# The order of turns, value products and projection pieces in the wide attentions of a four-layer kernel

## The chip, the core and the metric

The kernel runs on one core of a Trainium2 chip. The metric is the device time of one execution in microseconds. The core's engines are TensorE (PE for its matmuls, PEld for its weight loads), VectorE (DVE), ScalarE (ACT), GpSimd (POOL) and the DMA queues started by SyncE (SP).

## What is computed

Four layers, each a cross attention to a context followed by a mixture of experts or feed-forward network, on 16 batches of 112 tokens of width 256; the context has 375 rows. The change concerns the attentions of layers 2 and 3, cut here to their core (layer 3 adds biases to q, k, v and the output):

```python
qh = (q @ Wq).reshape(B_, Sq, 16, 64).transpose(0, 2, 1, 3)
kh = (k @ Wk).reshape(B_, Sk, 16, 64).transpose(0, 2, 1, 3)
vh = (v @ Wv).reshape(B_, Sk, 16, 64).transpose(0, 2, 1, 3)
scores = jnp.einsum('bhqd,bhkd->bhqk', qh, kh) / jnp.sqrt(jnp.float32(D_K))
attn = jax.nn.softmax(scores, axis=-1)
ctx = jnp.einsum('bhqk,bhkd->bhqd', attn, vh)
return ctx.transpose(0, 2, 1, 3).reshape(B_, Sq, 1024) @ Wo
```

## The kernel before

`cross_attention` emits one stage for each of layers 0, 2 and 3. In layers 2 and 3 the heads are 64 wide, so `EC`, the number of 128-row blocks of keys, is 8 and `wide` is true; in layer 0 it is false. There is no scheduler: each engine has a function of its own that walks the batches and heads in an order written out by hand, and semaphores tie them together.

For each batch and **pair** of heads (h even, h + 1) TensorE does these things:

- **scores** (S, L470): six matmuls of 376 columns, for both heads, into the two banks `psS`. It waits until ACT's exponentials have emptied both banks.
- **turn** (T, L497): three transposes that turn one head's weighted probabilities into the one bank `psT`. It waits for GpSimd's weighing of that head (`weighed`) and for ACT's copy of the previous head's turn (`probsT_ready`), since there is one bank.
- **pair_values** (PV, L512): twelve matmul records, the product of the turned probabilities of two heads with the values.
- **pieces** (`piece`, from L389): projections for the next batch and the output product of the last one. K0 to K7 are blocks of keys (six matmuls of 376 columns, L416), V0 to V5 blocks of values (six of 512 columns, L423), Q0 and Q1 queries (L408), L0 and L1 two transposes of the normed tokens (L401), Y0 and Y1 the output product of the batch before (L451). The dictionary `order` tells behind which head each stands.

Before the change a pair reads on TensorE, with h even:

S(h, h+1), T(h-3), pieces of h, T(h-2), PV(h-4, h-3), pieces of h+1.

The eight pairs of a batch hold these pieces, those of h before the bar and those of h+1 behind it: K0 K1 | K2; K3 | L0 L1 K4; V0 | V1; Y0 | V2; Y1 | K5; Q0 | V3; Q1 | V4; K6 | V5 K7.

The other engines, per pair: DVE takes the two maxima (`head_max`, L866). ACT copies T(h-3) (`take_probsT`, L654), exponentiates h and h+1 (L674), takes the pieces of h, copies T(h-2), and takes the pieces of h+1. GpSimd weighs every head (`weigh`): the inverse of the sum (L716), then the multiplication by it (L718). At head 8 it first starts the gathers of expert rows for a later batch (`gather`, L736): two in layer 2, one in layer 3, for the first twelve batches.

A K piece goes through two engines. ACT writes its high part (`keys_hi`, L626) and DVE then its low part (`keys_lo`, L808), and only then is its bank free. K pieces alternate between two banks of their own, so K2 waits for DVE to be done with K0, and K4 for K2. In the first pair DVE also starts the norm of the next batch (`normalise_start`) behind the maxima and ahead of K0. In the second pair, behind the maxima, it ends it (`normalise_end`, L788), and L0 waits for that.

What the four `probs` and four `probsT` buffers are read by sets the distances: T three and two heads behind the scores, PV four behind.

## Time and profile before

| | us |
|---|---|
| median of 3 runs | 3487.58 |
| lowest and highest | 3485.43, 3488.54 |
| the profiled execution | 3493.50 |
| its span, first to last instruction | 3491.7 |
| stage of layer 2's heads | 1515.9 to 2201.0 of the span |
| stage of layer 3's heads | 2477.7 to 3173.2 of the span |

The profile is of one execution. A timeline row has the start in microseconds from the start of the span, the duration, the engine, the line, the operation, what it writes from what, the shape, how many instructions were merged, and in brackets idle time of the engine before it with what ended it. The end of a matmul is modelled, so distances on TensorE are taken from start to start. A windows row has the stretch, its length, the busy time of PE, PEld, DVE, ACT and POOL with instruction counts, the granted TensorE clock as a share of the full one, the DMA share and GB/s.

### The profile page before, as it was taken

To read this page: it belongs to the slowest core of one execution; us is meant where nothing else is said; L and a number is where in the kernel's file an instruction comes from. 1 tells how busy PE (TensorE), PEld (TensorE's weight loads), DVE (VectorE), ACT (ScalarE), POOL (GpSimd) and SP (SyncE) were. 2 spreads that over 40 slices of the span, in tenths; PEclk is the share of its full clock that TensorE was granted. 3 is DMA by queue.
4 is the path that set the end of the run, shared out by engine and by line. 5 is a ranking of instruction groups with operands and counts; after the bars stand their busy time and mean duration, and the time that the engine had idled before them with its cause. 6 is when DMAs were issued, how large, how long until landed. Compare 5 with 4: busy or idle time off the path is not lost. (4 is left out here: it accounts for less than half of the span.)

```text
span 3491.7 us, 60671 instructions
## 1 busy us (share of the span) xinstructions
PE 3171.1 (91%) x21982; PEld 2617.9 (75%) x21982; DVE 1555.4 (45%) x3343; ACT 1527.9 (44%) x4145; POOL 1308.9 (37%) x1417
## 2 busy tenths in 40 slices
PE   5888869998989869989999999699899999996999
PEld 4777758996666646668888887588788888875998
DVE  4777750004566520044444444300444444445766
ACT  2555524443355512245555555234455555552332
POOL 0000001113100011057777776310577777773343
PEclk8999959999999879999999999699999999997999
DMA  6556536542100234110000000298000000001433
GB/s 145 131 133 137 118 130 204 182 166 82 38 1 1 88 93 119 60 32 15 15 15 15 15 13 1 77 320 276 27 13 13 13 13 13 11 1 44 120 103 90
DMA packets 154741, 269.25 MB, mean 77 GB/s; under 512 B 50396, under 2 KB 129753, under 8 KB 140393
## 3 DMA queue, kind: packets, MB, share of 16 engines
q1 hardware_dynamic: 140840, 239.95, 23.2%
q0 software_dynamic: 8064, 20.20, 2.2%
q10 hardware_dynamic: 5568, 5.51, 0.5%
q8 instruction: 172, 2.82, 0.3%
q14 instruction: 97, 0.79, 0.1%
HBM read 231.13 MB, written 34.46 MB: 76 GB/s over the span
## 5 line engine op out<-in xcount | busy, mean ns | idle before, releaser
L718 POOL TENSOR_SCALAR L_probs<-L_probs,L_inverse 112x375 f32<-112x375 f32 x512 | 653.0, 1275 | 119.5 <-issue 119.5
L866 DVE TENSOR_REDUCE L_negmax<-bank 112x1 f32<-112x375 f32 x768 | 394.6, 542 | 431.7 <-PE bank L470 356.9
L674 ACT ACTIVATE L_probs<-bank,L_negmax 112x375 f32<-112x375 f32 x768 | 435.2, 572 | 219.6 <-DVE L_negmax L866 214.7
L497 PE MATMUL bank<-ident,L_probs 112*125 112x112 f32 x2304 | 399.6, 282 | 21.2 <-POOL L_probs L718 15.4
L497 PEld LDWEIGHTS bank<-ident,L_probs 112*125 112x125 f32 x2304 | 338.8, 190 | 92.6 <-issue 50.9
L716 POOL TENSOR_TENSOR L_inverse<-L_sums,neg_one 112x1 f32<-112x1 f32 x512 | 297.1, 580 | 142.2 <-ACT L_probs L674 141.8
L654 ACT ACTIVATE L_probsT<-bank 125x336 f32<-125x336 f32 x512 | 231.9, 453 | 248.1 <-PE bank L497 248.1
L636 ACT ACTIVATE v<-bank 125x512 f32<-125x512 f32 x192 | 114.8, 598 | 267.4 <-PE bank L423 267.4
L704 POOL TENSOR_TENSOR L_stats<-L_stats,neg_half 112x1 f32<-112x1 f32 x48 | 27.1, 564 | 517.7 <-DVE L_stats L783 517.7
L512 PE MATMUL bank<-L_probsT,v 125*64 125x112 f32 x3072 | 206.1, 269 | 2.4 <-ACT L_probsT L654 1.1
L416 PE MATMUL bank<-L_ctx_hi,L_wk_hi 128*128 128x376 f32 x512 | 149.3, 373 | 29.8 <-DVE L_ctx_lo L850 22.1
L512 PEld LDWEIGHTS bank<-L_probsT,v 125*64 125x64 f32 x3072 | 151.5, 137 | 31.5 <-issue 2.7
L1582 ACT ACTIVATE L0t_hidden<-bank,L0t_b 128x128 f32<-128x128 f32 x280 | 102.3, 367 | 143.1 <-PE bank L1547 125.4
L674 ACT ACTIVATION_READ_ACCUMULATOR L_probs<-bank,L_negmax 112x1 f32 x768 | 152.9, 199 | 0.0
L1547 PEld LDWEIGHTS bank<-L0t_xT,L0t_w 128*128 128x128 f32 x1120 | 133.3, 195 | 5.9 <-issue 4.2
L423 PE MATMUL bank<-L_wv_hi,L_ctx_hi 128*125 128x512 f32 x384 | 137.7, 440 | 0.0
L1547 PE MATMUL bank<-L0t_xT,L0t_w 128*128 128x128 f32 x1120 | 133.8, 279 | 3.5 <-DMA L0t_w<-in_F_w 2.4
L808 DVE SCALAR_TENSOR_TENSOR L_keys_lo<-bank,L_bk,L_keys_hi 128x376 fp32r<-128x376 f32 x128 | 76.4, 606 | 130.8 <-ACT L_keys_hi L626 130.8
L416 PE MATMUL bank<-L_ctx_hi,L_wk_lo 128*128 128x376 f32 x512 | 131.6, 339 | 0.0
L416 PE MATMUL bank<-L_ctx_lo,L_wk_hi 128*128 128x376 f32 x512 | 131.3, 338 | 0.0
L1520 POOL DMA_INDIRECT L0t_xs<-tokens,rows_of x35 | 33.4, 955 | 256.6 <-PE bank L1533 209.7
L1598 DVE TENSOR_TENSOR L0t_ys<-bank,L0t_b 128x256 f32<-128x256 f32 x35 | 14.9, 424 | 253.9 <-PE bank L1559 253.9
(305 smaller groups left out, 6968.0 us busy)
## 6 DMA issues: line engine op xcount, KB each, us to landing
L2t_w<-in_F_w SPq DMA_DIRECT2D x42, 1024.0 KB, 5.1
L0t_w<-in_F_w SPq DMA_DIRECT2D x35, 1024.0 KB, 5.0
L_keys<-spread_k SPq DMA_DIRECT2D x64, 376.0 KB, 6.4
L_ctxT<-in_ctxT SPq DMA_DIRECT2D x48, 375.0 KB, 3.3
tile_w<-in_F_w SPq DMA_DIRECT2D x16, 1024.0 KB, 5.8
L3d_row<-comb_rows SPq DMA_DIRECT2D x64, 224.0 KB, 3.3
w_all<-in_F_w SPq DMA_DIRECT2D x8, 1024.0 KB, 13.6
L_q<-spread_q SPq DMA_DIRECT2D x128, 56.0 KB, 2.2
```

The source lines that it names most:

```text
L416: ins = pe.matmul(bank[:, 0:SP], wt[:, k, m * P:(m + 1) * P], c[b.par][:, k, :], start=(n + k == 0), stop=(n + k == DC + 1))
L423: ins = pe.matmul(bank[0:SJ, 0:VW], c[b.par][:, k, j * SJ:(j + 1) * SJ], wt[:, k, vn * VW:(vn + 1) * VW], start=(n + k == 0), stop=(n + k ...
L497: ins = pe.transpose(psT[h % len(psT)][0:SJ, j * T:(j + 1) * T], probs[h % NB][:, j * SJ:(j + 1) * SJ], core.ident[0:T, 0:T])
L512: ins = pe.matmul(bank[i * dh:(i + 1) * dh, at:at + T], v[b.par][0:SJ, j, (h + i) * dh:(h + i + 1) * dh], probsT[(h + i) % NT][:, j, :], s ...
L636: ins = act.activation(v[b.par][0:SJ, j, n * VW:(n + 1) * VW], bank[0:SJ, 0:VW], ACT.Copy)
L654: act.activation(probsT[h % NT][:, :, :], psT[h % len(psT)][0:SJ, 0:J * T].rearrange("p (j t) -> p j t", t=T), ACT.Copy)\
L674: act.activation(probs[e % NB][:, :], psS[e % 2][0:T, 0:S], ACT.Exp, bias=negmax[b.par][:, e:e + 1], accum_out=sums[b.par][:, e:e + 1]).th ...
L716: pool.tensor_tensor(inverse[b.par][:, h:h + 1], sums[b.par][:, h:h + 1], core.neg_one[0:T, :], ALU.pow)
L718: pool.tensor_scalar(probs[h % NB][:, :], probs[h % NB][:, :], inverse[b.par][:, h:h + 1], None, ALU.mult)\
L866: dve.tensor_reduce(negmax[b.par][:, h:h + 1], psS[h % 2][0:T, 0:S], AX, ALU.max, negate=True).then_inc(maxed.sem, 1)
L1547: ins = pe.matmul(psH[f % 4][:, 0:tile], w1[t % 2][:, k, f * P:(f + 1) * P], xT[:, k, :], start=(k == 0), stop=(k == DC - 1))
L1582: act.activation(hidden[:, f, :], psH[f % 4][:, 0:tile], func, bias=b1[:, bass.ds(e, 1), f:f + 1].rearrange("p a f -> p (a f)"))\
```

## The change

In wide attentions only:

- Both turns of a pair stand behind the scores with one value product between them. A pair reads S(h, h+1), T(h-3), PV(h-6, h-5), T(h-2), then the pieces of h and those of h+1.
- The value product is of a pair two heads older than before. The tail gets one more product for that.
- ACT copies T(h-2) between the two exponentials, where it stood behind the pieces of h.
- In `order` the first half of the second pair becomes L0 L1, and K3 and K4 stand together behind them. All other pairs keep their pieces. DVE's and GpSimd's functions are not edited.

```diff
     if wide:
-        order = {0: ["K0", "K1"], 1: ["K2"], 2: ["K3"], 3: ["L0", "L1", "K4"], 4: ["V0"], 5: ["V1"], 6: ["Y0"],
+        order = {0: ["K0", "K1"], 1: ["K2"], 2: ["L0", "L1"], 3: ["K3", "K4"], 4: ["V0"], 5: ["V1"], 6: ["Y0"],
                  7: ["V2"], 8: ["Y1"], 9: ["K5"], 10: ["Q0"], 11: ["V3"], 12: ["Q1"], 13: ["V4"],
                  14: ["K6"], 15: ["V5", "K7"]}
...
                         scores(b, h)
-                        if not (b_first and h < lag):
+                        if wide and h % 2 == 0:
+                            if not (b_first and h < 3):
+                                turn(*before(b, h, 3))
+                            if not (b_first and h < 6):
+                                pair_values(*before(b, h, 6))
+                            if not (b_first and h < 2):
+                                turn(*before(b, h, 2))
+                        if not wide and not (b_first and h < lag):
                             turn(*before(b, h, lag))
-                        if wide and h % 2 == 1 and not (b_first and h < 5):
-                            pair_values(*before(b, h, 5))
...
                     if wide:
                         turn(b, H - 3)
+                        pair_values(b, H - 6)
                         turn(b, H - 2)
                         pair_values(b, H - 4)
...
-                        if wide and not (b_first and h < lag):
-                            take_probsT(*before(b, h, lag))
+                        if wide and h % 2 == 0 and not (b_first and h < 3):
+                            take_probsT(*before(b, h, 3))
 
                         for e in ((h, h + 1) if h % 2 == 0 else ()) if wide else (h,):
+                            if wide and e == h + 1 and not (b_first and h < 2):
+                                take_probsT(*before(b, h, 2))
                             act.wait_ge(maxed.sem, maxed.at(H * b.n + e + 1))
```

TensorE in the second pair of a batch before the change. L497 is a turn, L512 the value product, L401 the transposes L0 and L1, L416 with `wk_hi` and `wk_lo` a K piece:

```order
L470 MATMUL bank<-L_keys_hi,L_q_low 112x376 x2
L497 MATMUL bank<-ident,L_probs 125x112 x3
L416 MATMUL bank<-L_ctx_hi,L_wk_hi 128x376 x2
L416 MATMUL bank<-L_ctx_lo,L_wk_hi 128x376 x2
L416 MATMUL bank<-L_ctx_hi,L_wk_lo 128x376 x2
L497 MATMUL bank<-ident,L_probs 125x112 x3
L512 MATMUL bank<-L_probsT,v_3 64x112 x6
L401 MATMUL bank<-ident,L_normed 128x112 x2
L416 MATMUL bank<-L_ctx_hi,L_wk_hi 128x376 x2
```

The same place after the change:

```order
L470 MATMUL bank<-L_keys_hi,L_q_low 112x376 x2
L497 MATMUL bank<-ident,L_probs 125x112 x3
L512 MATMUL bank<-L_probsT,v_3 64x112 x6
L497 MATMUL bank<-ident,L_probs 125x112 x3
L401 MATMUL bank<-ident,L_normed 128x112 x2
L416 MATMUL bank<-L_ctx_hi,L_wk_hi 128x376 x2
L416 MATMUL bank<-L_ctx_lo,L_wk_hi 128x376 x2
L416 MATMUL bank<-L_ctx_hi,L_wk_lo 128x376 x2
L416 MATMUL bank<-L_ctx_hi,L_wk_hi 128x376 x2
```

K3, which stood ahead of L0, now stands behind L1, and nothing but the two turns and the product stands between the scores and L0.

ACT over the first two pairs of a batch before the change: L654 is the copy of a turn, L674 the exponential, L626 the high part of a K piece, L624 the copy of L0 and L1:

```order
L654 ACTIVATE L_probsT<-bank 125x336
L674 ACTIVATE L_probs,L_sums<-bank,L_negmax 112x375 x2
L626 ACTIVATE L_keys_hi<-bank 128x376 x2
L654 ACTIVATE L_probsT<-bank 125x336
L626 ACTIVATE L_keys_hi<-bank 128x376
L654 ACTIVATE L_probsT<-bank 125x336
```

After it, with the line numbers of the changed kernel (L660 copy of a turn, L682 exponential, L632 high part of a K piece):

```order
L660 ACTIVATE L_probsT<-bank 125x336
L682 ACTIVATE L_probs,L_sums<-bank,L_negmax 112x375
L660 ACTIVATE L_probsT<-bank 125x336
L682 ACTIVATE L_probs,L_sums<-bank,L_negmax 112x375
L632 ACTIVATE L_keys_hi<-bank 128x376 x3
L660 ACTIVATE L_probsT<-bank 125x336
```

The second copy of a turn moved from behind the pieces of h to between the exponentials, and the three K pieces of the first pair are taken in a row.

## Rows read from the trace of the kernel before

**Rows 1.** Windows of layer 2's and layer 3's head stages.

```profile
1515.90:2201.00 685.10, 671.28 (x5267) 547.69 (x5269) 312.30 (x647) 359.50 (x999) 492.80 (x543) 1.00 0.05 13
2477.70:3173.20 695.50, 681.64 (x5354) 557.14 (x5354) 315.93 (x635) 376.83 (x1008) 502.57 (x555) 0.99 0.04 10
```

**Rows 2.** Timeline of PE, layer 3, first two pairs of the sixth batch.

```profile
2693.84 0.43 PE L470 MATMUL bank<-L_keys_hi,L_q_high 64*112 64x376 f32 x2
...
2694.53 0.58 PE L497 MATMUL bank<-ident,L_probs 112*125 112x112 f32 x3
2694.88 0.60 PE L416 MATMUL bank<-L_ctx_hi,L_wk_hi 128*128 128x376 f32 x2
...
2696.00 0.51 PE L416 MATMUL bank<-L_ctx_hi,L_wk_hi 128*128 128x376 f32 x2
...
2697.03 0.48 PE L497 MATMUL bank<-ident,L_probs 112*125 112x112 f32 x3
2697.45 0.80 PE L512 MATMUL bank<-L_probsT,v 125*64 125x112 f32 x12
2698.17 0.62 PE L416 MATMUL bank<-L_ctx_hi,L_wk_hi 128*128 128x376 f32 x2
...
2699.40 0.42 PE L470 MATMUL bank<-L_keys_hi,L_q_high 64*112 64x376 f32 x2
...
2701.96 0.80 PE L512 MATMUL bank<-L_probsT,v 125*64 125x112 f32 x12
2702.69 0.41 PE L401 MATMUL bank<-ident,L_normed 112*128 112x112 f32 x2
...
2704.07 0.42 PE L470 MATMUL bank<-L_keys_hi,L_q_high 64*112 64x376 f32 x2
```

**Rows 3.** Timeline of PE, layer 2, first pair of the sixth batch.

```profile
1736.58 0.43 PE L470 MATMUL bank<-L_keys_hi,L_q_high 64*112 64x376 f32 x2
...
1741.15 0.62 PE L416 MATMUL bank<-L_ctx_hi,L_wk_hi 128*128 128x376 f32 x2 [0.16 <-DVE L_keys_lo L808]
...
1742.38 0.42 PE L470 MATMUL bank<-L_keys_hi,L_q_high 64*112 64x376 f32 x2
```

**Rows 4.** Timelines of ACT (layer 3), DVE (layer 3), DVE (layer 2), second pairs.

```profile
2700.71 0.45 ACT L654 ACTIVATE L_probsT<-bank 125x336 f32<-125x336 f32 x1 [0.63 <-PE bank L497]
...
2701.55 0.59 DVE L788 TENSOR_SCALAR L_normed<-x,L_stats 112x256 f32<-112x256 f32 x1
...
1744.38 0.40 DVE L788 TENSOR_SCALAR L_normed<-x,L_stats 112x256 f32<-112x256 f32 x1
```

**Rows 5.** Timelines of PE and DVE, K pieces in a row, layer 3's start, then layer 2's.

```profile
2459.10 0.61 PE L416 MATMUL bank<-L_ctx_hi,L_wk_hi 128*128 128x376 f32 x2 [0.29 <-DVE L_keys_lo L808]
...
2461.71 0.61 PE L416 MATMUL bank<-L_ctx_hi,L_wk_hi 128*128 128x376 f32 x2 [0.28 <-DVE L_keys_lo L808]
...
2461.04 0.61 DVE L808 SCALAR_TENSOR_TENSOR L_keys_lo<-bank,L_bk,L_keys_hi 128x376 fp32r<-128x376 f32 x1 [0.97 <-ACT L_keys_hi L626]
...
1498.53 0.62 PE L416 MATMUL bank<-L_ctx_hi,L_wk_hi 128*128 128x376 f32 x2
...
1501.00 0.61 PE L416 MATMUL bank<-L_ctx_hi,L_wk_hi 128*128 128x376 f32 x2
```

**Rows 6.** Timeline of PEld, layer 2's first batch: two turns with nothing between them.

```profile
1533.53 0.40 PEld L497 LDWEIGHTS bank<-ident,L_probs 112*125 112x125 f32 x3 [0.26 <-issue]
1534.71 0.40 PEld L497 LDWEIGHTS bank<-ident,L_probs 112*125 112x125 f32 x3 [0.78 <-POOL L_probs L718]
```

**Rows 7.** Timelines of PE and POOL, layer 2, sixth pair (heads 10, 11), two batches.

```profile
1763.11 0.42 PE L470 MATMUL bank<-L_keys_hi,L_q_high 64*112 64x376 f32 x2
...
1764.41 1.24 POOL L718 TENSOR_SCALAR L_probs<-L_probs,L_inverse 112x375 f32<-112x375 f32 x1 [2.29 <-issue]
...
1631.63 0.42 PE L470 MATMUL bank<-L_keys_hi,L_q_high 64*112 64x376 f32 x2
...
1631.69 1.24 POOL L718 TENSOR_SCALAR L_probs<-L_probs,L_inverse 112x375 f32<-112x375 f32 x1 [1.05 <-issue]
```

## The prediction, made before the changed kernel ran

> **What bounds the kernel now.** I read a window over each of the two stages that the change touches, then TensorE's timeline inside one batch. In the two stages TensorE is busy for 671.3 of 685.1 us and 681.6 of 695.5 us at a granted clock of 1.00 and 0.99 [rows 1]. GpSimd follows with 492.8 and 502.6 us. So nearly all of these 1380.6 us are TensorE's own work, and whatever the change does to the time it must do by the seams between TensorE's blocks or by new waits of TensorE. That is the upper of its two levels (2.4 GHz), so nothing is to be had from the clock.
>
> A timeline of TensorE, read from start to start, gives the price of each block with its seam. In layer 3's first pair: S 0.69 us, T 0.35, K0 1.12, K1 1.03, T 0.42, PV 0.72, K2 1.23, together 5.56 [rows 2]. The second pair takes 4.67 us: its PV starts at 2701.96 and L0 at 2702.69, again 0.73, and L0, L1, K4 take 1.38 up to the next scores [rows 2]. Layer 2's first pair takes 5.80 us, and its K2 is the one block that waits there: 0.16 us idle, ended by DVE's low part of K0 [rows 3].
>
> **The seams.** A turn behind the scores costs 0.58 us of modelled duration, one behind a K piece 0.48 [rows 2]: the first has 0.10 more because its weight loads do not run ahead. K0 behind a turn costs 1.12, K1 behind K0 1.03; K2 behind a value product has its first two matmuls in 0.62 where K1 has 0.51 [rows 2]. So a block in the wake of a turn or product pays about 0.1, and one behind a K piece does not.
>
> Before, the first pair pays at S-T, T-K, T-PV and PV-K, and K-T is free. After, it pays at S-T, T-PV, PV-T and T-K, and K-K is free. The seam PV-T does not occur in the rows, so I bound it. The nearest is PV-L0, another fp32 transpose with `ident`: 0.73 for the product with its seam [rows 2]. The other end is what the seam costs if the turn's load runs ahead as behind a K piece: the turn is then 0.10 cheaper, and the product's own 0.72 may shrink by about the same again. I take 0.72 and 0.10, the PV-L0 row being the same kind of instruction. Then the first pair is S 0.69, T 0.35 + 0.10 + 0.06 = 0.51 (a turn that leads to PV is 0.42 against 0.35, and this one also stands behind scores), PV 0.72, T 0.35, K0 1.12, K1 1.03, K2 1.23 - 0.11 = 1.12, in all 5.54 against 5.56. **The seams cancel.** The second pair comes out the same way at about 4.72 against 4.67, since K3 and K4 follow two small transposes. The other six pairs have V, Y or Q pieces at the same places; I take 0 for them, with 0.05 us either way per pair. Over six pairs and 30 batches (15 with pieces in each layer) that is 9 us up or down.
>
> **The copy of the first turn.** T(h-2) needs the one `psT` bank back, so ACT must have copied T(h-3). Before, a piece of over 1 us stood between them. Now the product does. In layer 2's first batch, where two turns stand back to back, the second one's weights load 1.18 us after the first's [rows 6]: that is turn, copy and signal. After the change the distance is 0.51 + 0.72 = 1.23 us. So the wait is covered, by 0.05 us. The copy starts 0.62 us behind its turn (2700.71 against 2699.40 + 0.69) and takes 0.45, and ACT sat idle for 0.63 us before it [rows 2, 4], so nothing stands in front of it. I cost it at 0, with up to 0.05 per pair, 12 us, as the upper end.
>
> **K2 in the first pair.** Three K pieces now stand in a row, and K2 needs K0's bank. Where K pieces stand in a row, the start of one to the start of the next but one is 2.61 us in layer 3 and 2.47 us in layer 2, ended by DVE's low part [rows 5]; without the wait it would be 1.12 + 1.03 = 2.15. Before, a turn and a product stood in between. K0 now starts 0.69 + 0.51 + 0.72 + 0.35 = 2.27 us into the pair, so K2 starts at 4.88 (layer 3) and 4.74 (layer 2), and with K2's 1.23 the pair takes 6.11 and 5.97 us. Against 5.56 and 5.80 [rows 2, 3] that is 0.55 and 0.17 us more, over 15 batches 8.3 + 2.6 = **10.9 us**. ACT copies T(h-2) from 1.92 + 0.62 = 2.54 to 2.99 us and has then the second exponential ahead of K0's high part, while K0 is made only at about 3.5 (2.27, 1.12 and some 0.1 for the last matmul to end, an estimate). I take it that ACT is there in time; if it were late by 0.1 us, that would be 3 us more.
>
> **L0 in the second pair.** L0 waits for DVE's normed tokens. In layer 3 these are done at 2701.55 + 0.59 = 2702.14 [rows 4], 2.74 us after the pair's start at 2699.40 [rows 2], and the signal from DVE to TensorE takes 0.06 us (DVE ends at 2461.65, the K piece starts at 2461.71 [rows 5]), so L0 can start at 2.80. Nothing on DVE ahead of that moves: K2's low part and the two maxima stand there before and after. Before, L0 came at 2702.69, 3.29 us in, and was safe. After, it would come at 0.69 + 0.51 + 0.72 + 0.41 = 2.33. It waits 0.47 us, and its weight load no longer runs ahead, 0.05. With the 0.05 of the seams the pair is 0.57 us longer. In layer 2 the tokens are done at 1744.78, 2.40 us into a pair that starts at 1742.38 [rows 3, 4]: a wait of 0.13, and 0.2 us in all. Together 15 x (0.57 + 0.2) = **11.5 us**.
>
> **T(8) behind the gathers, layer 2.** GpSimd weighs head 8 behind two gathers, and the multiplication ends 2.54 us after the scores of heads 10 and 11 start in one batch (1765.65 against 1763.11) and 1.30 us in another [rows 7]. Twelve batches have gathers, and these two are near the two ends of what they show. T(8) is the second turn of that pair. Before, it stood behind Q0, a piece longer than a microsecond. Now it stands at 0.69 + 0.51 + 0.72 = 1.92 us. It waits 0.68 in the one and nothing in the other; I take 0.46 on average, **5.5 us**, bounds 2 and 8. In layer 3, with one gather, I see no such wait.
>
> **What costs nothing.** S(h+2) waits for the second exponential. It now starts when the copy ends at 2.99, and the shortest pair is 4.67, which leaves 1.7 us. DVE's copies of the value products stand behind maxima that end later than the product. In the last batch of each stage, with few pieces, GpSimd sets the pace and the extra product in the tail lies in its shadow.
>
> **The sum.** 10.9 + 11.5 + 5.5 = 27.9 us more. Against the profiled execution's own 3493.5 that is 3521.4; against the median of 3487.6, which I forecast for, 3515.5, so about **3515**. From the bounds (seams -9 to +9, copy 0 to +12, T(8) -3.5 to +2.5, ACT 0 to +3) its own range is 3503 to 3530.
>
> **Rivals.** (a) *The product hides the turn's loads.* If TensorE loads T(h-2)'s weights while the product still runs, both ends of the seam PV-T shrink, 0.1 to 0.2 us for each of 240 pairs: 24 to 48 us less. With 36 us, the sum is -8 and the time 3480, faster by 0.23%. It decides the sign from 0.12 us per pair on. For it speaks that a K piece does hide a turn's loads [rows 2]; against it that the loads of K2 and L0 are not hidden behind a product. Chance 0.10. The Trainium skill (TensorE: Matmul & The Clock Gate, "Step-by-step: what each phase is for") says that the queue pulls weight loads ahead of matmuls in flight when the row groups don't conflict or the load goes to the background buffer; by that rule this rival would hold. The trace agrees behind K pieces but not behind the product. (b) *The copy is late.* With 0.1 us of wait per pair for `psT`, 24 us more: 3539. The margin of 0.05 us is thin, but the first batch's row includes all of the chain. Chance 0.10. (c) *The new waits find slack I have not seen*: if L0 or K2 does not wait, one of the two large terms falls away, and the time is about 3504 with one and 3493 with neither. Against it stands that layer 2 already shows K2's wait [rows 3]. Chance 0.15 for one, 0.05 for both.
>
> **How the numbers follow.** My forecast has 0.60. The range of 3490 to 3535 holds it, (c) and a part of (b), and leaves out (a) and most of (b), 0.2. A measurement of this kernel can tell about 0.2%, 7 us, from no change: faster 0.08 (most of (a)), same 0.09 (the rest of (a), and (c) with both gone), slower 0.83.
>
> **What would show it.** In the changed profile each first pair should be 6.1 us in layer 3 and 6.0 in layer 2, K2 idle before its loads, ended by DVE's low part; each second pair 5.2 and 4.9 us, L0's load ended by DVE's normed tokens; T(8) in layer 2 ended by GpSimd; PV to the second turn 0.72 us; the other pairs within 0.05 us of before. I am wrong if PV-T is near 0.6 or less, if second turns wait for ACT's copy throughout, or if K0's copy on ACT stands much behind the end of K0.

## The result, and the profile after

The changed kernel takes 3525.4 us (median of 4 runs, 3520.4 to 3535.6) where the kernel before takes 3488.1 (median of 4 runs, three of them those of the table above). The comparison of the runs gives 1.0096 of the time before, with a 95% interval of 1.0073 to 1.0119; the quotient of the two medians alone would be 1.0107. **It is slower, by 0.7 to 1.2%.** The forecast of 3515 is 1.0079 of 3487.6, inside that interval, and 3525.4 lies in the range of 3490 to 3535. The profiled run of after took 3525.82 us with a span of 3524.0; that of before had a span of 3491.7.

Windows over the two stages from the first scores to the last (length, busy us and instructions of PE, PEld, DVE, ACT, POOL, granted clock, DMA share, GB/s), layer 2 and layer 3 of after, then the same two stretches of before, which end some us earlier than those of [rows 1]:

```profile
1514.70:2215.50 700.80, 682.27 (x5255) 552.30 (x5255) 314.45 (x647) 372.58 (x999) 494.25 (x546) 0.99 0.05 12
2494.10:3193.30 699.20, 680.33 (x5253) 551.50 (x5254) 313.31 (x631) 387.98 (x999) 498.18 (x548) 0.99 0.04 10
```
```profile
1515.90:2200.80 684.90, 671.08 (x5267) 547.49 (x5267) 312.30 (x647) 359.50 (x999) 492.60 (x543) 1.00 0.05 13
2477.70:3155.60 677.90, 668.81 (x5267) 546.52 (x5267) 314.01 (x631) 373.47 (x999) 494.83 (x547) 1.00 0.04 11
```

The stages are 15.9 and 21.3 us longer, 37.2 in all. The rest of the span went the other way by 5: 1.2 us less ahead of layer 2's stage, 1.6 more between the two, 5.4 less behind the second. The change touches none of these, so I put them down to variation. Of the 37.2, TensorE's busy time has grown by 22.7 (682.27 + 680.33 less 671.08 + 668.81) and its idle time by 14.5. Nearly the same instructions were busy longer; I put that down to modelled durations next to waits and to a lower clock in places.

Next, the starts of the scores, from which every pair has a length. The table has after less before, summed over the 14 batches between the first and the last of each stage (from the two profiled runs, us):

| | pair 1 | 2 | 3 | 4 | 5 | 6 | 7 | 8 | sum of 14 | first batch | last batch | stage |
|---|---|---|---|---|---|---|---|---|---|---|---|---|
| layer 2 | +2.1 | +5.0 | -0.1 | +0.1 | -0.2 | +3.5 | -1.9 | -0.3 | +8.3 | +4.3 | +3.3 | +15.9 |
| layer 3 | +7.3 | +7.1 | -0.1 | +0.1 | -0.2 | +0.2 | -0.9 | -0.2 | +13.3 | +7.2 | +0.9 | +21.4 |

So 21.5 us come from the regular batches, in the pairs and layers that the sum named (first, second, and layer 2's sixth). Another 15.7 come from the two first and two last batches, which the sum had all but left out.

**The regular batch.** TensorE's timeline in layer 3's sixth batch (start, duration, line, tiles; a bracket is idle time and what ended it); it answers to [rows 2]:

```profile
2721.27 0.42 PE L470 MATMUL bank<-L_keys_hi,L_q_high 64*112 64x376 f32 x2
...
2721.97 0.58 PE L497 MATMUL bank<-ident,L_probs 112*125 112x112 f32 x3
2722.48 0.80 PE L512 MATMUL bank<-L_probsT,v 125*64 125x112 f32 x12
2723.20 0.58 PE L497 MATMUL bank<-ident,L_probs 112*125 112x112 f32 x3
2723.55 0.60 PE L416 MATMUL bank<-L_ctx_hi,L_wk_hi 128*128 128x376 f32 x2
...
2724.68 0.50 PE L416 MATMUL bank<-L_ctx_hi,L_wk_hi 128*128 128x376 f32 x2
...
2726.15 0.62 PE L416 MATMUL bank<-L_ctx_hi,L_wk_hi 128*128 128x376 f32 x2 [0.29 <-DVE L_keys_lo L816]
...
2727.38 0.42 PE L470 MATMUL bank<-L_keys_hi,L_q_high 64*112 64x376 f32 x2
...
2729.30 0.58 PE L497 MATMUL bank<-ident,L_probs 112*125 112x112 f32 x3
2730.08 0.41 PE L401 MATMUL bank<-ident,L_normed 112*128 112x112 f32 x2 [0.19 <-DVE L_normed L796]
...
2732.56 0.43 PE L470 MATMUL bank<-L_keys_hi,L_q_high 64*112 64x376 f32 x2
```

The first pair takes 6.11 us (2727.38 - 2721.27), the second 5.18. K2 starts 1.47 behind K1, where K1 itself follows K0 by 1.13, and its wait is ended by DVE's low part of K0. L0 starts 0.78 behind the second turn, which takes 0.35 when K0 follows it. From the product's start to the second turn's it is 0.72 (2722.48 to 2723.20), the number taken from PV to L0.

DVE in layer 3 and layer 2, and TensorE's L0 in layer 2:

```profile
2729.53 0.40 DVE L796 TENSOR_SCALAR L_normed<-x,L_stats 112x256 f32<-112x256 f32 x1
...
1750.40 0.40 DVE L796 TENSOR_SCALAR L_normed<-x,L_stats 112x256 f32<-112x256 f32 x1
```
```profile
1750.95 0.41 PE L401 MATMUL bank<-ident,L_normed 112*128 112x112 f32 x2
```

In both layers L0 starts 0.15 us after DVE is done (2729.93 to 2730.08, 1750.80 to 1750.95).

**Layer 2's sixth pair**, TensorE and GpSimd in the sixth batch, to be laid beside [rows 7]:

```profile
1769.48 0.43 PE L470 MATMUL bank<-L_keys_hi,L_q_high 64*112 64x376 f32 x2
...
1771.87 0.58 PE L497 MATMUL bank<-ident,L_probs 112*125 112x112 f32 x3 [0.39 <-POOL L_probs L726]
...
1775.56 0.43 PE L470 MATMUL bank<-L_keys_hi,L_q_high 64*112 64x376 f32 x2
```
```profile
1770.57 1.24 POOL L726 TENSOR_SCALAR L_probs<-L_probs,L_inverse 112x375 f32<-112x375 f32 x1 [2.52 <-issue]
```

T(8) stands 2.39 us into its pair, where 1.94 is its place without a wait, and the pair takes 6.08 instead of 5.63. Over the 11 middle batches with gathers the pair takes 5.71 to 6.38.

**The first batch of a stage** is another matter. Windows of after, layer 3's first batch, its second and its sixth pair, then the sixth pair of before (the window begins 0.06 us early):

```profile
2500.26:2507.29 7.03, 6.30 (x25) 5.11 (x24) 2.45 (x5) 3.02 (x9) 6.44 (x7) 0.53 0.00 0
2520.10:2531.70 11.60, 8.66 (x47) 7.29 (x47) 2.54 (x5) 2.50 (x7) 8.05 (x9) 0.71 0.14 44
```
```profile
2502.30:2508.00 5.70, 5.70 (x47) 4.58 (x47) 2.54 (x5) 2.71 (x7) 4.55 (x5) 1.00 0.28 75
```

The sixth pair takes 11.60 us instead of 5.64. TensorE of before in the fourth pair of that batch, of after in its fourth and sixth, and GpSimd of after in the sixth:

```profile
2495.22 0.55 PE L497 MATMUL bank<-ident,L_probs 112*125 112x112 f32 x3 [0.63 <-ACT L_probsT L654]
```
```profile
2514.48 0.58 PE L497 MATMUL bank<-ident,L_probs 112*125 112x112 f32 x3
...
2525.04 0.97 PE L497 MATMUL bank<-ident,L_probs 112*125 112x112 f32 x3 [2.93 <-POOL L_probs L726]
2525.80 3.62 PE L408 MATMUL bank<-L_hT,wq 128*128 128x112 f32 x16
```
```profile
2523.74 1.24 POOL L726 TENSOR_SCALAR L_probs<-L_probs,L_inverse 112x375 f32<-112x375 f32 x1 [2.23 <-issue]
```

A first batch has few pieces. Before, two turns stood back to back in its fourth and fifth pairs, and the second waited 0.63 us for ACT's copy of the first. The product now stands between them, so these two pairs are 0.85 and 0.65 us shorter (4.71 to 3.86, 4.35 to 3.70). That is a gain of its own, but TensorE gets ahead of GpSimd with it and gives it back and more: T(8) waits 2.93 us for the weighing behind the gather. The granted clock falls at the end of that wait and stays at its lower level (1.2 GHz) until about 2531.5: the Q piece, 1.95 us for 16 matmuls elsewhere, takes 3.62.

**The last batch.** TensorE and ACT of after in layer 2's last batch, then TensorE of before, one such pair:

```profile
2190.68 0.42 PE L470 MATMUL bank<-L_keys_hi,L_q_high 64*112 64x376 f32 x2 [1.19 <-ACT L_probs L682]
...
2194.38 0.43 PE L470 MATMUL bank<-L_keys_hi,L_q_high 64*112 64x376 f32 x2 [1.19 <-ACT L_probs L682]
```
```profile
2189.53 0.45 ACT L660 ACTIVATE L_probsT<-bank 125x336 f32<-125x336 f32 x1 [0.22 <-PE bank L497]
2189.87 0.57 ACT L682 ACTIVATE L_probs<-bank,L_negmax 112x375 f32<-112x375 f32 x1
```
```profile
2178.70 0.42 PE L470 MATMUL bank<-L_keys_hi,L_q_high 64*112 64x376 f32 x2
...
2181.81 0.42 PE L470 MATMUL bank<-L_keys_hi,L_q_high 64*112 64x376 f32 x2
```

With no pieces in the pair the scores now wait 1.19 us for the second exponential, which stands on ACT behind the copy of the second turn. The pair takes 3.70 us (2190.68 to 2194.38) and took 3.11. The waits of the whole stage of layer 3, after and then before (us in total, times, longest), show the exchange:

```profile
PE bank L416 <- DVE L_keys_lo L816: 5.8, 15, 1.9
PE bank L470 <- ACT L_probs L682: 4.7, 4, 1.2
PE bank L401 <- DVE L_normed L796: 3.2, 15, 0.6
PE bank L497 <- POOL L_probs L726: 3.1, 2, 2.9
PE bank L497 <- ACT L_probsT L660: 0.6, 1, 0.6
```
```profile
PE bank L497 <- POOL L_probs L718: 4.1, 4, 1.4
PE bank L497 <- ACT L_probsT L654: 2.5, 4, 0.6
PE bank L416 <- DVE L_keys_lo L808: 2.1, 2, 1.9
```

K2 now waits 15 times instead of twice and L0 15 times, the scores wait for ACT four times, and the turn waits for ACT's copy once instead of four times.

### The profile page after: what moved, and what is told of

Its sections match the earlier page's. It is cut to its first block and busy times, and to the rows that moved or that the text cites. A ratio compares the mean times of both kernels' runs of the same rounds, so it can differ in the third digit from the quotient of the medians.

```text
span 3524.0 us, 60671 instructions
## 1 busy us (share of the span) xinstructions
PE 3193.3 (91%) x21982; PEld 2632.2 (75%) x21982; DVE 1562.1 (44%) x3343; ACT 1555.7 (44%) x4145; POOL 1306.0 (37%) x1417
## 5 line engine op out<-in xcount | busy, mean ns | idle before, releaser
L682 ACT ACTIVATE L_probs<-bank,L_negmax 112x375 f32<-112x375 f32 x768 | 438.4, 571 | 218.1 <-DVE L_negmax L874 212.3
L497 PE MATMUL bank<-ident,L_probs 112*125 112x112 f32 x2304 | 426.5, 295 | 12.6 <-POOL L_probs L726 9.1
L497 PEld LDWEIGHTS bank<-ident,L_probs 112*125 112x125 f32 x2304 | 332.3, 191 | 118.1 <-issue 58.0
L660 ACT ACTIVATE L_probsT<-bank 125x336 f32<-125x336 f32 x512 | 231.1, 451 | 245.9 <-PE bank L497 242.2
L512 PE MATMUL bank<-L_probsT,v 125*64 125x112 f32 x3072 | 209.0, 272 | 1.1 <-ACT L_probsT L660 1.1
L416 PE MATMUL bank<-L_ctx_hi,L_wk_hi 128*128 128x376 f32 x512 | 147.0, 369 | 32.7 <-DVE L_ctx_lo L858 22.0
L512 PEld LDWEIGHTS bank<-L_probsT,v 125*64 125x64 f32 x3072 | 152.9, 139 | 29.6 <-ACT L_probsT L660 1.6
L682 ACT ACTIVATION_READ_ACCUMULATOR L_probs<-bank,L_negmax 112x1 f32 x768 | 152.4, 198 | 0.0
L416 PE MATMUL bank<-L_ctx_hi,L_wk_lo 128*128 128x376 f32 x512 | 132.3, 340 | 0.0
L416 PE MATMUL bank<-L_ctx_lo,L_wk_hi 128*128 128x376 f32 x512 | 131.7, 339 | 0.0
L408 PE MATMUL bank<-L_hT,wq 128*128 128x112 f32 x1024 | 127.9, 280 | 0.9 <-ACT L_hT L630 0.9
L451 PE MATMUL bank<-wo,L_oT 128*112 128x128 f32 x1024 | 127.1, 279 | 1.6 <-DVE L_oT L890 0.8
```

Of the source, the lines that this page charges most:

```text
L408: ins = pe.matmul(bank[:, (c - 4 * m) * T:(c - 4 * m + 1) * T], wq[:, k, c * P:(c + 1) * P], hT[:, k, :], start=(k == 0), stop=(k == DC - 1))
L416: ins = pe.matmul(bank[:, 0:SP], wt[:, k, m * P:(m + 1) * P], c[b.par][:, k, :], start=(n + k == 0), stop=(n + k == DC + 1))
L497: ins = pe.transpose(psT[h % len(psT)][0:SJ, j * T:(j + 1) * T], probs[h % NB][:, j * SJ:(j + 1) * SJ], core.ident[0:T, 0:T])
L512: ins = pe.matmul(bank[i * dh:(i + 1) * dh, at:at + T], v[b.par][0:SJ, j, (h + i) * dh:(h + i + 1) * dh], probsT[(h + i) % NT][:, j, :], s ...
L660: act.activation(probsT[h % NT][:, :, :], psT[h % len(psT)][0:SJ, 0:J * T].rearrange("p (j t) -> p j t", t=T), ACT.Copy)\
L682: act.activation(probs[e % NB][:, :], psS[e % 2][0:T, 0:S], ACT.Exp, bias=negmax[b.par][:, e:e + 1], accum_out=sums[b.par][:, e:e + 1]).th ...
```

## Experiments

The theory: three waits make the loss, each because the change took a piece from ahead of a block that is fed by another engine (K2 from DVE by way of K0's bank, L0 from DVE's normed tokens, T(8) from GpSimd behind the gathers), and the seams are worth nothing. The rival: the new order itself costs at its seams, or the loss lies in something else that an undone wait would not give back. Each ratio below is against the kernel before on the same chip, with its 95% interval; pair lengths are from the profiled run.

**The change again.** No edit: what one profile of the same kernel differs from another by.

> The changed kernel as it is, beside the runs of its undoings. All theories expect 1.0096 of the kernel before again (3520 to 3536 us). In the trace: first pairs 5.96 us in layer 2 and 6.10 in layer 3, second pairs 5.03 and 5.19. What differs from run to run should be the granted clock in the first batch of each layer, where TensorE waits.

3527.5 us, 1.0098 (1.0065 to 1.0131). Regular batches cost +9.1 and +13.4 us over 14 (+8.3 and +13.3 in the first profile). Layer 2's last batch took 31.0 us instead of 28.5, with one pair of 7.45 that is elsewhere 4.19. Regular batches can be compared between two profiles to about 1 us over 14; a last batch alone cannot.

**L0 behind K3.** Against the changed kernel:

```
-        order = {0: ["K0", "K1"], 1: ["K2"], 2: ["L0", "L1"], 3: ["K3", "K4"], 4: ["V0"], 5: ["V1"], 6: ["Y0"],
+        order = {0: ["K0", "K1"], 1: ["K2"], 2: ["K3"], 3: ["L0", "L1", "K4"], 4: ["V0"], 5: ["V1"], 6: ["Y0"],
```

K3 goes back between the second turn and L0, and the piece that follows L1 is K4 as before the change.

> The changed kernel with the second pair's pieces in the old order K3, L0, L1, K4. Theory: L0 waits for DVE's normed tokens and this alone makes the second pair 5.03 and 5.19 us; with K3 ahead it falls to about 4.72 in both layers, 14 to 15 x (0.31 + 0.47), 11 to 12 us less than the changed kernel, and up to 3 us more from the first batches. Rival: the new seams make the second pair long, then it stays above 4.95 and the time moves by under 3 us.

3516.4 us, 1.0057 (1.0037 to 1.0078): against the change on the same chip 11 us less by the medians and 14 by the ratios. TensorE in layer 3's second pair, which starts at 2720.66:

```profile
2722.59 0.58 PE L497 MATMUL bank<-ident,L_probs 112*125 112x112 f32 x3
2722.94 0.58 PE L416 MATMUL bank<-L_ctx_hi,L_wk_hi 128*128 128x376 f32 x2
...
2724.05 0.36 PE L401 MATMUL bank<-ident,L_normed 112*128 112x112 f32 x2
...
2725.39 0.42 PE L470 MATMUL bank<-L_keys_hi,L_q_high 64*112 64x376 f32 x2
```

L0 waits for nothing. The pair takes 4.73 us in both layers, where before it took 4.69 and 4.68. Over 14 batches that leaves +0.6 of the +5.0 and +7.1. So the loss of L0's wait is shown for the regular batches. In layer 3's first batch the second pair takes 4.16 us at a granted clock of 1.00, against 7.03 at 0.53 in the change, but layer 2's takes 6.51 at 0.51 here too. That the first batches' loss is L0's is therefore not shown (more on this below).

**K0 and K1 ahead of the second turn, in the first pair alone.**

```
+                            if h == 0:
+                                for p, d in pieces_at(0, b_first, b_last):
+                                    at, (prior, pd) = where[p] if not b_last else last_where[p]
+                                    piece(p, b + d, (at, (prior, b + pd)))
                             if not (b_first and h < 2):
                                 turn(*before(b, h, 2))
...
-                        for p, d in pieces_at(h, b_first, b_last):
+                        for p, d in pieces_at(h, b_first, b_last) if not (wide and h == 0) else ():
...
-                            if wide and e == h + 1 and not (b_first and h < 2):
+                            if wide and e == h + 1 and h > 0:
...
+                        if wide and h == 0 and not b_first:
+                            take_probsT(*before(b, 0, 2))
```

ACT copies that turn behind the high parts of K0 and K1.

> The changed kernel with, in the first pair alone, K0 and K1 between the value product and the second turn (and ACT's copy of that turn behind K0 and K1), K2 behind the turn. Theory: three K pieces in a row wait for the bank of K0; with a turn between, K2's wait shrinks by 0.35 us, and ACT takes K0 0.3 us earlier: first pair about 5.7 in layer 3 (from 6.10) and 5.85 in layer 2 (from 5.96), 6 to 8 us less. Rival: the first pair is long from its seams, then it stays above 6.0 in layer 3.

3521.0 us, 1.0079 (1.0054 to 1.0103), 6.5 us less than the change on the same chip. The first pairs take 5.79 and 5.77 us. Over 14 batches layer 2's first pair is back at the length before (0.0 instead of +2.1), layer 3's at +2.7 instead of +7.3. The 0.2 us per pair that are left in layer 3 are K2's wait again, not a seam. K2 starts 0.05 us after DVE's low part of K0 in every regular batch, 2.61 us behind K0 (2713.82 to 2716.43) as in [rows 5], and 0.44 behind the turn, where a piece follows a turn that stands behind a piece in 0.25 (as in the third pair of the order that pays, further down). The two turns without a wait would take 0.51 + 0.25 us, as much as the 0.35 + 0.42 of before [rows 2].

**Both gathers one head later**, at head 9 instead of 8, so that GpSimd weighs head 8 ahead of them:

```
-                        if h == 8 and b.n + 4 < B:
+                        if h == 9 and b.n + 4 < B:
```

> The changed kernel with GpSimd's gathers started ahead of head 9's weighing instead of head 8's. Theory: T(8), now the second turn early in the sixth pair, waits for the weighing behind the gathers, in layer 2 in most of 12 batches (0.3 us in the mean) and in both layers' first batches (11.6 us pairs at a clock of 0.71 instead of 7.4 and 5.6). With the gathers one head later T(8) is ready, T(9) is needed only in the next pair: sixth pairs 5.64 in all batches, 4 us from the steady ones and up to 12 from the first ones, so 8 to 16 us less than the changed kernel. Rival: the first batches' 11.6 us come from elsewhere (the clock alone), then they stay and the time falls by 4 us or less.

3549.1 us, 1.0161 (1.0131 to 1.0190): **slower than the change, where 8 to 16 us less were expected.** What it was meant to do it did. Layer 2's sixth pairs take 5.64 us, and the first batches 45.9 and 45.0 us instead of 49.5 and 49.1. But layer 2's seventh pairs cost 16.8 us over 14 batches: GpSimd now weighs heads 9 and 10 behind the gathers, and the two turns of that pair both wait. At head 8 the gathers had run in a time in which GpSimd waited for the exponentials anyway: in this kernel the weighing of head 8 waits 1.65 us for ACT (the inverse at 1777.11). The same in layer 3, with one gather, costs nothing in a regular batch (-0.9 as in the change). The profiles do not locate all of the 22 us (16 between the two profiled runs, of this kernel and of the change run again): 7 lie in the regular and first batches, 4 in the last ones and 5 outside the two stages, and the last two parts are not explained.

**The gathers apart**, one at head 8 and one at head 10, and in the first batch at 12 and 14:

```
-                        if h == 8 and b.n + 4 < B:
-                            gather(b.n + 4)
+                        at = h - (12 if b_first else 8)
+                        if at in (0, 2) and at // 2 < topk and b.n + 4 < B:
+                            gather(b.n + 4, (at // 2,))
...
-                    for k in range(topk):
+                    for k in ks or range(topk):
```

> The changed kernel with the two gathers of layer 2 split, one ahead of head 8's weighing and one ahead of head 10's, and in each layer's first batch moved to heads 12 and 14. Theory: T(8) waits because two gathers stand ahead of head 8's weighing; one alone does not make it wait (layer 3's steady sixth pairs are at 5.64 us). And moving both behind head 8 delayed heads 9 and 10, since they then miss GpSimd's idle time. So the sixth pair should be 5.64 in layer 2 too, no pair longer for it, 4 us from the steady batches, and the first batches 44 to 45 us instead of 49: 10 to 14 us less than the changed kernel in all. Rival: any gather at heads 8 to 10 costs what it takes, then seventh pairs grow by what the sixth ones lose and the gain is that of the first batches alone.

3529.9 us, 1.0094 (1.0067 to 1.0121): no gain. TensorE in a seventh pair of layer 2 that starts at 1784.03, and GpSimd ahead of it:

```profile
1786.51 0.58 PE L497 MATMUL bank<-ident,L_probs 112*125 112x112 f32 x3 [0.47 <-POOL L_probs L726]
```
```profile
1781.25 1.02 POOL L745 DMA_INDIRECT L_got<-slots_out,slot_out  x1 [0.17 <-issue]
...
1785.21 1.24 POOL L726 TENSOR_SCALAR L_probs<-L_probs,L_inverse 112x375 f32<-112x375 f32 x1 [2.31 <-issue]
```

From the gather's start to the next head's multiplication it is 3.96 us on GpSimd, 2.31 of them an idle time that nothing in the trace ends, and T(10) waits for that multiplication's end. The sixth pairs are back (+0.2), the seventh cost 10.5 us over 14. The first batches take 43.7 and 43.2 us, 5.8 and 5.9 less than in the change: the wait of 2.93 us behind the gather, with the clock that it took along, is shown to be that much of them.

**The same split in the kernel before**, as a control:

> The kernel before with the gathers split and moved as in a5_gathers_split. Theory: before the change head 8's weighing kept TensorE waiting only in layer 2's first batch (1.8 us), so the ratio is 0.999 to 1.000, and what a5 gains is a cost that the change brought. Rival: the gathers cost the kernel before as much, then 0.997 or less.

3496.3 us beside 3493.5, 1.0004 (0.9992 to 1.0016). Where the pieces still stand between the turns, neither place of the gathers costs or gives anything that the times can tell. The profile shows one exception: layer 2's first batch has a sixth pair of 7.44 us before and of 5.64 here. So T(8)'s wait belongs to the change in all batches but that one, where the change made it longer (11.60).

**The three edits together** (L0 behind K3, K0 and K1 early, gathers apart at 8 and 10):

> The changed kernel with the three waits taken away at once: K3 ahead of L0 and L1, K0 and K1 ahead of the second turn in the first pair, the gathers split as in the run before. Theory: the new seams are worth nothing either way, and the three waits are the whole loss: 12 to 14, 6 to 7 and 10 to 14 us less than the changed kernel, so within 5 us of the kernel before (ratio 0.998 to 1.002). Rival: part of the loss is in the seams or in ACT's copy between the exponentials, then it stays at 1.004 or more.

3505.7 us, 1.0050 (1.0028 to 1.0072), where at most 1.002 was expected. Layer 3's regular batches are at +2.3 us over 14, layer 2's at +10.3, and 9.7 of these are the seventh pair with the gather at head 10. The miss is that gather's, known from the run above.

**The same with the second gather at head 12:**

```
-                        at = h - (12 if b_first else 8)
-                        if at in (0, 2) and at // 2 < topk and b.n + 4 < B:
-                            gather(b.n + 4, (at // 2,))
+                        at = [12, 14] if b_first else [8, 12]
+                        if h in at[0:topk] and b.n + 4 < B:
+                            gather(b.n + 4, (at.index(h),))
```

> As a6_three_undone, but layer 2's second gather stands ahead of head 12's weighing instead of head 10's (in the first batches at heads 12 and 14 as there). In a6 T(10) waited for it: seventh pairs of 6.18 us in the median and up to 9.4 instead of 5.64. Theory: head 12 has the slack that head 10 lacks, so all sixth and seventh pairs of layer 2 are 5.64, the batches 43.8 us and the first ones 42: about 9 us less than a6 (3496 beside 3505), ratio 1.001 to 1.003 of the kernel before; what is left is 0.2 us in each first pair of layer 3 and nothing in the seams. Rival: the wait moves on to head 14 or 0 and the ratio stays at 1.004 or more.

3489.6 us beside 3495.7, 0.9994 (0.9974 to 1.0013). **The whole loss is gone**, and there is no gain that can be told from none. The regular batches stand at -1.4 and +2.3 us over 14 against before, the first batches at -2.0 and -0.8, the last at +1.0 and +3.5. In seven of the eight pairs of a batch the product still stands alone between the turns, all pieces stand behind the second turn, and ACT's copy stands between the exponentials. So that order by itself is worth nothing (within the interval, -9 to +5 us), as the forecast had it, and the three waits with their followers were the loss.

**An order that does pay.** In the kernel before, a value product leads to a piece or to L0. If it stood last in its pair, it would lead to the next scores, and the piece would follow the turn:

```
-                        if wide and h % 2 == 1 and not (b_first and h < 5):
-                            pair_values(*before(b, h, 5))
...
                             piece(p, b + d, (at, (prior, b + pd)))
+                        if wide and h % 2 == 1 and not (b_first and h < 5):
+                            pair_values(*before(b, h, 5))
```

> The kernel before with the value product moved behind the pieces of h+1, as the last block ahead of the next scores; nothing else is changed. Before, a pair pays for the seams S-T, T-piece, T-PV, PV-piece and piece-S. Here it would pay for S-T, T-piece, T-piece, piece-PV and PV-S. A product behind scores' neighbours costs 0.19 us from its last matmul to the next scores where a K piece costs 0.26. Theory that a seam costs whenever the shape of the array's tiles changes: piece-PV costs about as much as T-PV, the piece behind the second turn 0.1 less than behind the product, so 0.2 to 0.25 us per pair, 45 to 60 us less (ratio 0.983 to 0.988). Rival: piece-PV is dearer or the K pieces and the product's new place bring waits of their own, then the ratio is 0.995 or more.

3469.5 us, 0.9936 (0.9918 to 0.9954): faster than both kernels, by half of what was expected. Pairs 3 to 8 give 2.0 to 4.7 us each over 14 batches, and the second pair 1.8 and 2.1, but the first costs 6.2 and 5.9. TensorE in layer 3's first pair:

```profile
2682.31 0.48 PE L497 MATMUL bank<-ident,L_probs 112*125 112x112 f32 x3
...
2683.17 0.62 PE L416 MATMUL bank<-L_ctx_hi,L_wk_hi 128*128 128x376 f32 x2 [0.38 <-DVE L_keys_lo L808]
...
2684.40 0.80 PE L512 MATMUL bank<-L_probsT,v 125*64 125x112 f32 x12
2685.13 0.42 PE L470 MATMUL bank<-L_keys_hi,L_q_high 64*112 64x376 f32 x2
```

Taking the product from ahead of K2 brought K2's wait again: 0.86 us from the turn to K2. The product with its way to the scores takes 0.73, as it did to L0 [rows 2], so that seam is not cheaper. The gain of 0.17 us per pair stands at the turn: it led to the product in 0.42 us and leads to a piece in 0.25 in the third pair of this kernel.

**The same, but the product ahead of K2 in the first pair**, against the kernel before:

```
-                        if wide and h % 2 == 1 and not (b_first and h < 5):
+                        if wide and h == 1 and not b_first:
                             pair_values(*before(b, h, 5))
...
+                        if wide and h % 2 == 1 and h > 1 and not (b_first and h < 5):
+                            pair_values(*before(b, h, 5))
```

> As b2_pv_last (the kernel before with the value product as the last block of a pair), but in the first pair of a batch the product keeps its old place between the second turn and K2, since without it K2 waits for K0's bank: first pairs 6.24 and 6.00 us in b2 against 5.80 and 5.56 before. Theory: these come back and the other pairs stay at 5.05 to 5.75 (0.13 to 0.25 us less than before), so 13 us less than b2: about 3457 us beside 3488, ratio 0.990. Rival: the wait is not the product's cover, then the first pairs stay above 5.9 and the ratio at 0.9936.

3462.1 us beside 3495.7, 0.9906 (0.9890 to 0.9923). The first pairs take 5.56 us in both layers. The second now costs +0.6 and +3.0 over 14, 4.73 and 4.88 us: L0 comes early there and waits for the normed tokens.

**The same with K4 ahead of L0:**

```
-        order = {0: ["K0", "K1"], 1: ["K2"], 2: ["K3"], 3: ["L0", "L1", "K4"], 4: ["V0"], 5: ["V1"], 6: ["Y0"],
+        order = {0: ["K0", "K1"], 1: ["K2"], 2: ["K3"], 3: ["K4", "L0", "L1"], 4: ["V0"], 5: ["V1"], 6: ["Y0"],
```

> As b6_pv_last_but_first, but the second pair's pieces behind the second turn are K4, L0, L1 instead of L0, L1, K4. In b6, with the product no longer ahead of L0, L0 waits for DVE's normed tokens again (second pairs 4.73 in layer 2 and 4.88 in layer 3). Theory: with K4 ahead L0 comes a microsecond later and does not wait, second pairs about 4.5 in both layers, 15 x (0.2 + 0.35) = 8 us less than b6: ratio 0.988 to 0.989 of the kernel before. Rival: L0 and L1 directly ahead of the product cost seams of their own, then 0.9906 stays.

3451.2 us beside 3496.2, **0.9878 (0.9855 to 0.9902)**, the best of all. TensorE at the end of layer 3's second pair:

```profile
2673.58 0.35 PE L401 MATMUL bank<-ident,L_normed 112*128 112x112 f32 x2
2673.86 0.80 PE L512 MATMUL bank<-L_probsT,v 125*64 125x112 f32 x12
2674.59 0.43 PE L470 MATMUL bank<-L_keys_hi,L_q_high 64*112 64x376 f32 x2
```

The pair started at 2670.03 and takes 4.56 us. Over the two stages this kernel stands at -22.5 and -18.5 us against before, 41 of the 45 measured.

## Why the prediction came out, point by point

**K2's wait: right.** The first pairs were forecast at 5.97 and 6.11 us and have medians of 5.96 and 6.10. Over 14 batches they cost 2.1 + 7.3 = 9.4 us, where the step gives 10.1 for 14. The experiment on it alone gave back what was expected, though it left 0.2 us per pair of K2's wait in layer 3. ACT was in time.

**L0's wait: right in kind, and its two sizes were off in opposite ways.** The second pairs were forecast at 5.24 (layer 3) and 4.9 (layer 2) and have medians of 5.19 and 5.03. The sum gave 0.57 and 0.2 per batch; measured are +7.1 and +5.0 over 14, so 0.51 and 0.36. The signal from DVE was taken as 0.06 from a K piece; L0 takes 0.15 after DVE's end. In layer 3 the normed tokens took 0.40 us where [rows 4] has 0.59, which is more than the signal cost. In layer 2 they took 0.40 both times, and the error of the signal remained. Why they took longer before in layer 3 is open. With 12.1 over 14 batches against 10.8, the term was 1.3 short.

**T(8) in layer 2: right in kind, too high.** 3.5 us over the 11 middle batches with gathers, where 0.46 each gives 5.1. The ends from [rows 7] were right (0 and 0.68; measured 0.08 to 0.76), but 0.46 was taken for the mean where their middle is 0.34 and the 11 batches measured 0.32.

**The seams: right.** PV to T is 0.72 us, as taken, and T behind the scores 0.51. Pairs 3 to 8 without layer 2's sixth come to -3.5 us over 28 batches, inside the -9 to +9. Half of that is layer 2's seventh pair (-1.9), as short in the kernel with the waits undone: in the sixth batch of before the product of that pair starts 0.60 us behind its turn instead of 0.42, and the change takes this away.

**Rival (a) fell.** The product does not hide the second turn's weight loads. They start with the turn's matmuls at 2729.30, where behind a K piece of before they start 0.16 us ahead (2696.87 for the turn at 2697.03):

```profile
2729.30 0.40 PEld L497 LDWEIGHTS bank<-ident,L_probs 112*125 112x125 f32 x3
```

Hidden loads would have shown 0.5 to 0.6 from PV to T in place of 0.72, and the undone kernel with the product between the turns would have been faster by 24 to 48 us. It was within 0.2% of before. So the rule quoted there (the Trainium skill, TensorE: Matmul & The Clock Gate, "Step-by-step: what each phase is for") held behind K pieces and not behind this product, as the rows of before had it.

**Rival (b) fell** too: in the regular batch the second turn does not wait for ACT's copy. The row of [rows 6] that the margin was taken from names GpSimd's weighing, but the matmuls of that turn were released by the copy, so the chain was read rightly:

```profile
1534.75 0.55 PE L497 MATMUL bank<-ident,L_probs 112*125 112x112 f32 x3 [0.63 <-ACT L_probsT L654]
```

(c) fell with the two waits: both came.

**What was missed: the short batches.** This was the sum's real fault: 15.7 of the 37.2 us. Two steps of the text failed.

"In layer 3, with one gather, I see no such wait": true of regular batches alone. In the first batch of each stage the pairs ahead of the sixth became shorter by 1.5 us, since the product filled a wait for ACT's copy. TensorE came to T(8) with the gather still running, waited 2.93 us in layer 3, and then worked at the lower clock. Moving the gathers in that batch gave back 5.8 and 5.9 us.

The second pair of that batch lost another 2 to 3 us (+2.0 in layer 2, +2.9 in layer 3). It goes with the lower clock, and its cause stays open. In layer 3 the granted clock is 0.51 to 0.55 over that pair in all five profiles in which L0 waits (6.85 to 7.03 us), and 1.00, 0.82 and 0.79 in the three in which K3 stands ahead of it (4.16 to 4.29 us; in two of them the clock fell in the first pair already, which takes 6.99 and 6.85 us instead of 6.15). But L0's wait did not make the clock fall. In the changed kernel the turn at 2501.42 already takes 0.97 us instead of 0.58, L0's wait comes behind it, from 2502.40 to 2502.97, and the lower level lasts to about 2507. In layer 2 the pair is as long in two of the three kernels with K3 ahead (6.5 us at 0.51), is short in one in which L0 waits (5.04 at 1.00), and before the change its clock fell too (0.70, 4.72 us) but came back within the pair.

"In the last batch [...] GpSimd sets the pace and the extra product lies in its shadow" failed too, along with "leaves 1.7" for the second exponential. That margin was worked out for the shortest regular pair, of 4.67 us. A pair without pieces lasted 3.11, and the exponential that starts at 2.99 and takes 0.57 us cannot be done by then. The scores wait 1.19 us, and such pairs take 3.70. The first three pairs of the two last batches cost 1.5 and 1.4 us more than before. The whole of these batches stands at +3.3 and +0.9, but 1.4 of the 3.3 is layer 2's seventh pair alone, of 5.32 us at a granted clock of 0.53. No experiment undid the wait alone, and the last batch varies by some us between profiles of one kernel.

The forecast total came out within its bounds partly because errors went against each other: the regular batches cost 21.5 us where the three terms give 26.0 over 14 (10.1, 10.8, 5.1), the short ones 15.7 where they give 2.0, and the rest of the span was 5 us shorter. The sum's own range was also added up wrongly. Its lower end is right, but +9, +12, +2.5 and +3 on 3515.5 make 3542 and not 3530; the range that was forecast, 3490 to 3535, held the result all the same.

## What to carry to other kernels

A block that needs another engine's result lives on whatever stands ahead of it. Before pieces are regrouped, list for each such block when its input is ready, measured from the start of the period, and its new place: where the second is the smaller, the difference is lost in every period, and a K piece put back ahead of it costs nothing. Do the same list for the first and last period of a loop, which have fewer pieces: a margin worked out in the full period is not there, and time saved in front of a wait can be given back with the clock on top. And an order pays by what leads to what: here a turn that leads to a projection piece instead of to the product is worth about 0.17 us per pair, once K2 and L0 are kept fed (0.9878).

## What the runs showed of the hardware

- **The way from a released wait to the first matmul depends on what waits.** K pieces started 0.06 us after DVE's end [rows 5], the two small transposes 0.15 us after it, in both layers.
- **A gather costs GpSimd more than its own row.** The instruction takes 1.02 us, but the next multiplication starts 3.96 us after the gather does, with 2.31 us in between of which the trace names no end. In the kernel with the gathers apart this distance is 2.9 to 3.0 us in layer 3's regular batches and 2.9 to 5.5 in layer 2, mostly about 4. Where a gather stands among GpSimd's work therefore matters: with two of them one head later, layer 2's seventh pairs cost 16.8 us over 14 batches instead of -1.9, in a kernel where GpSimd is busy only 37% of the span.
- **A wait of about 3 us in a stage at full clock was followed by the lower level.** In layer 3's first batch the granted clock is 1.00 up to 2524, 0.76 over the last microsecond of the wait, 0.50 from 2525 to 2531 and 1.00 again from 2532; TensorE's Q piece takes 3.62 instead of 1.95 us. Of the 5.95 us that the pair lost, 2.93 are the wait, and most of the rest is the clock.
